# Scores of the diagonal packed into whole PSUM banks, products with V in four batches a group, eight slots for the weights

## The reference

```
mod = silu(c) @ wmod -> sa, ca, ga, sb, cb, gb          (ga, gb pushed away from zero)
h   = layernorm(x) * (1 + ca) + sa
x   = x + ga * (softmax_causal(Q K^T / 4) V @ Wo^T + bo)     with Q, K, V = h @ Wqkv^T + b
h   = layernorm(x) * (1 + cb) + sb
x   = x + gb * sum over the 2 chosen experts e of w_e * (silu(h @ w1[e]) @ w2[e])
```

## Time and profile before

| | |
|---|---|
| median of 3 runs | 999.07 us |
| span of the profiled execution | 997.7 us |
| TensorE busy (matmuls) | 902.3 us, 90% |
| VectorE busy | 718.0 us, 72% |
| ScalarE busy | 580.5 us, 58% |
| GpSimd busy | 357.4 us, 36% |

### The profile page before, as it was taken

One profiled execution on the slowest core, in us unless ns is written; L12 is line 12 of the kernel. 1 busy time (PEld: TensorE's weight loads), 2 busy tenths in 40 slices (PEclk: granted clock), 3 DMA queues, 4 the chain that ended last, 5 costly groups with the idle time before them and its releaser, 6 DMA issues.

```text
span 997.7 us, 19445 instructions
## 1 busy us (share of the span) xinstructions
PE 902.3 (90%) x6174; PEld 531.5 (53%) x6174; DVE 718.0 (72%) x2323; ACT 580.5 (58%) x1271; POOL 357.4 (36%) x311
## 2 busy tenths in 40 slices
PE   5899899999899998999999897878899999999990
PEld 3543335433444443543443452423699899999980
DVE  8688766879656789757689669699638584444587
ACT  3335485776585777577666757567535433334562
POOL 1332020431321314333033454015386466565630
PEclk7899899999999999999999999999999999999995
DMA  8446436336326167251662745215313323222699
GB/s 282 127 65 129 61 81 144 59 44 146 63 35 133 42 112 142 69 76 59 106 115 85 152 64 189 73 27 174 96 53 123 95 70 106 78 75 71 198 309 306
DMA packets 83235, 110.61 MB, mean 111 GB/s; under 512 B 15930, under 2 KB 56434, under 8 KB 83138
## 3 DMA queue, kind: packets, MB, share of 16 engines
q1 hardware_dynamic: 75506, 89.45, 38.8%
q0 software_dynamic: 6816, 18.62, 6.1%
q10 hardware_dynamic: 816, 1.32, 0.4%
HBM read 69.42 MB, written 35.41 MB: 105 GB/s over the span
## 4 chain that ended last, share of the span: by engine, by line
PE 62%; DVE 16%; ACT 9%; issue 5%; DMA 4%; POOL 3%; SPq 1%; ACTq 0%; POOLq 0%; DVEq 0%
PE PO L1643 10%; PE PH L1520 9%; PE PY L1520 9%; PE PS L1623 8%; PE PM L1600 8%; ACT PR L1009 4%; DVE MXF L1322 3%; PE PHT L1728 3%; PE PX L1655 2%; PE PX L1569 2%; DVE JK L1319 2%; PE PS L1627 2%; PE PX L1578 2%; PE PX L1579 1%; ACT SF L992 1%
## 5 line engine op out<-in xcount | busy, mean ns | idle before, releaser
L1009 ACT ACTIVATE PR<-PS 128x512 f32<-128x512 f32 (+3 forms) x768 | 334.3, 497 | 142.4 <-PE PS L1627 108.1
L1319 DVE CUSTOM_DVE_ANT_0 JK<-PM,MK 128x128 bf16<-128x128 f32 (+3 forms) x512 | 239.1, 484 | 54.0 <-PE PM L1600 52.8
L1600 PE MATMUL PM<-QK 128*128 128x512 bf16 (+3 forms) x768 | 249.1, 333 | 23.4 <-DVE MXF L1322 15.0
L1623 PE MATMUL PS<-QK 128*128 128x512 bf16 (+3 forms) x768 | 247.5, 333 | 10.4 <-ACT PR L1009 7.4
L1322 DVE TENSOR_REDUCE MXF<-PM 128x1 f32<-128x512 f32 x256 | 175.1, 684 | 83.2 <-PE PM L1600 81.6
L1623 PEld LDWEIGHTS PS<-QK 128*128 128x128 bf16 x768 | 75.0, 98 | 170.4 <-ACT PR L1009 107.8
L1643 PE MATMUL PO<-PR,V 128*17 128x512 f32 (+3 forms) x1536 | 162.8, 496 | 0.0
L1600 PEld LDWEIGHTS PM<-QK 128*128 128x128 bf16 x768 | 75.5, 99 | 98.0 <-DVE MXF L1322 36.8
L1520 PE MATMUL PY<-W2S,HT 128*128 x852 | 118.9, 289 | 2.8 <-issue 1.9
L1520 PE MATMUL PH<-W1S,XT 128*128 x426 | 113.3, 402 | 0.9 <-DVE W2S L1474 0.9
L1627 PE MATMUL PS<-MT,identb 128*128 128x128 bf16 x512 | 111.9, 221 | 0.0
(11 more groups left out here) (269 smaller groups left out, 1194.9 us busy)
## 6 DMA issues: line engine op xcount, KB each, us to landing
QK<-SD SPq DMA_DIRECT2D x180, 128.0 KB
SD<-SP SPq DMA_DIRECT2D x42, 256.0 KB, 2.8
OP<-OS SPq DMA_DIRECT2D x64, 64.0 KB
LP<-LR SPq DMA_DIRECT2D x64, 64.0 KB
W1S<-in_w SPq DMA_DIRECT2D x8, 512.0 KB, 5.7
X<-XA SPq DMA_DIRECT2D x3, 1024.0 KB, 8.8
H2D<-XA SPq DMA_DIRECT2D x3, 1024.0 KB, 4.9
YG<-YT SPq DMA_DIRECT2D x12, 256.0 KB, 4.4
```

Of the source, the lines that this page charges most:

```text
L1009: eng.activation(PR[:, slot, i, c0:512], PS[m % 3][:, c0:512], ACT.Exp, scale=0.25).then_inc(S["exp"].sem, 1)
L1319: eng.tensor_tensor_reduce(JK[:, jk % 2, 0:w], PM[m % 3][:, 0:w], MK[:, 512 - w:512], 1.0, -3.0e38, ALU.add, ALU.max, MXA[:, mb, h, qt:qt ...
L1600: eng.matmul(PM[m % 3][:, 0:128 * (k1 - k0)], QK[:, r, h, 0, qt * 128:(qt + 1) * 128], QK[:, r, h, 1, k0 * 128:k1 * 128], start=True, stop ...
L1623: last = eng.matmul(PS[m % 3][:, c0:512], QK[:, r, h, 1, j * 128:(j + 1) * 128], QK[:, r, h, 0, 512 * f + c0:512 * f + 512], start=True, s ...
```

## The change

Eight key blocks of a group's 12 hold diagonal parts, of 512, 384, 256 and 128 columns a head. The change lists, for each half f: the key blocks up to 4f as before ("all", 512 columns); a slot kind "odd", whose bank holds a head's 384 columns of key block 4f+1 and behind them its 128 columns of block 4f+3; and a kind "two", whose bank holds the 256 columns of block 4f+2 for two heads. So a group has 18 slots (36 banks) in place of 24 (48 banks), and every exponential has 512 columns. The mask of "odd" and "two" is one matmul of 256 columns (for "two" with an output of two strips of 128). Score step n of a group stands where half step 48n/36 stands, maxima stay where they are. The products with V are made in 4 steps a group: key blocks 0 to 3 of half 0; blocks 0, 1 of half 1; blocks 2, 3; blocks 4 to 7. Each step waits once, for the last exponential of its batch, and stands LAG steps after its last score (steps 9, 14, 19 and 26 from the group's start; before, the 12 stood 2 steps apart at 4 to 26). `PR` has 8 slots, the last three at another place in SBUF; for their space the reserve for GpSimd's DMA descriptors is set to 4096. The unused `LATE` is taken out.

```diff
-SLOTS = 5
+SLOTS = 8
+FIRST_SLOTS = 5
-SCORES = [(f, j, p) for f in range(2) for j in range(4 * f + 4) for p in range(2)]
+SCORES = [slot for f in range(2) for slot in
+          [("all", f, j, p) for j in range(4 * f + 1) for p in range(2)] + [("odd", f, 1, p) for p in range(2)] + [("two", f, 2, 0)]]
+BATCHES = ((0, 5, (0, 1, 2, 3)), (5, 9, (0, 1)), (9, 13, (2, 3)), (13, 18, (4, 5, 6, 7)))
+def score_pieces(n, i):
+    kind, f, j, p = SCORES[n]
+    if kind == "all":
+        return [(2 * p + i, j, 0, 512, 0)]
+    if kind == "odd":
+        return [(2 * p + i, 4 * f + 1, 128, 512, 128), (2 * p + i, 4 * f + 3, 0, 128, 384)]
+    return [(2 * i, 4 * f + 2, 0, 256, 256), (2 * i + 1, 4 * f + 2, 256, 512, 256)]
...
-        for n, (f, j, p) in enumerate(SCORES):
-            if p == 1:
-                place(g, n + LAG - ahead(g, f), one("pv", g, f, j))
+        for n, (_, f, _, _) in enumerate(SCORES):
+            k = half_of("score", 2 * n + 1) // 2 - ahead(g, f)
+            b = batch_of(n)
+            if n == BATCHES[b][1] - 1:
+                place(g, k + LAG, one("pv", g, b))
...
# ScalarE, score
-                    if m // 2 >= SLOTS:
-                        ac.wait_ge(S["pv"], (m // 2 - SLOTS) // 2 + 1)
-                    eng.activation(PR[:, slot, i, c0:512], PS[m % 3][:, c0:512], ACT.Exp, scale=0.25).then_inc(S["exp"].sem, 1)
+                    if s >= SLOTS:
+                        ac.wait_ge(*after("pv", "pv", (s - SLOTS) // NS, batch_of((s - SLOTS) % NS)))
+                    eng.activation(PR[s % SLOTS][:, i, :], PS[m % 3][:, :], ACT.Exp, scale=0.25).then_inc(S["exp"].sem, 1)
...
# TensorE, score
-                    last = eng.matmul(PS[m % 3][:, c0:512], QK[:, r, h, 1, j * 128:(j + 1) * 128],
-                                      QK[:, r, h, 0, 512 * f + c0:512 * f + 512], start=True, stop=True)
+                    for piece, (h, j, c0, c1, q0) in enumerate(score_pieces(n, i)):
+                        q0 += 512 * f
+                        last = eng.matmul(PS[m % 3][:, c0:c1], QK[:, r, h, 1, j * 128:(j + 1) * 128],
+                                          QK[:, r, h, 0, q0:q0 + c1 - c0], start=piece == 0, stop=True, skip_group_check=True)
...
# TensorE, pv
-                    for i in range(4):
-                        last = eng.matmul(PO[32 * i:32 * i + 17, c0:512], V[g // 4 % 2][:, j, 4 * (g % 4) + i, :],
-                                          PR[:, (m - 1 + i // 2) % SLOTS, i % 2, c0:512], start=(j == 0), stop=(j == 4 * f + 3),
-                                          skip_group_check=True)
+                    for j in keys:
+                        for h in range(4):
+                            n, i, c0, c1, q0 = place_of(f, j, h)
+                            last = eng.matmul(PO[32 * h:32 * h + 17, q0:q0 + c1 - c0], V[g // 4 % 2][:, j, 4 * (g % 4) + h, :],
+                                              PR[ring_s["score", g, n, i] // 2 % SLOTS][:, i, c0:c1], start=(j == 0),
+                                              stop=(j == 4 * f + 3), skip_group_check=True)
...
-    nc = bacc.Bacc("TRN2", target_bir_lowering=False, num_devices=1)
+    nc = bacc.Bacc("TRN2", target_bir_lowering=False, num_devices=1, dynamic_dma_scratch_size=4096)
```

More of the change, by code:

```diff
@@ L83, in is_cut @@
 def is_cut(n):
-    f, j, _ = SCORES[n]
-    return j >= 4 * f
+    kind, f, j, _ = SCORES[n]
+    return kind != "all" or j == 4 * f
 def schedule():
@@ new lines, in schedule, with score_step, max_step @@
+    score_at = {half_of("score", n): n for n in range(2 * NS)}
+    def score_step(t, i):
+        w, k = divmod(t, nw)
+        if 1 <= w < NG and 2 * k + i in score_at:
+            n = score_at[2 * k + i]
+            return ("score", w, n // 2, n % 2)
+        for f in range(2):
+            n = score_at.get(2 * (t + AHEAD[f]) + i)
+            if n is not None and SCORES[n // 2][1] == f:
+                return ("score", 0, n // 2, n % 2)
+    def max_step(t, i):
+        g, m = divmod(t + LEAD, nw)
+        if 0 <= g < NG and 2 * m + i in max_at:
+            return ("max", g, max_at[2 * m + i])
@@ L227, in schedule @@
     for t in range(-3 * nw, NG * nw + LAG + 1):
         now[0] = t - 0.5
[L229 to L240, removed]
+        if score_step(t, 0):
+            order.append(score_step(t, 0))
+        elif (t + LEAD) // nw >= 0 and t < -AHEAD[0]:
@@ L247, in schedule @@
         now[0] = t
-        if score:
-            order.append(("score", *score, 1))
-        order += fill[1:]
+        if score_step(t, 1):
+            order.append(score_step(t, 1))
+        if max_step(t, 1):
+            order.append(max_step(t, 1))
         while at.get(t):
@@ L312 @@
 NR = len(ROUTE[0])
-LATE = ()
 RING = 10
@@ L502, in adaln_block @@
         TM = sb("TM", [128, 2, D], F32, att)
+        PRB = sb("PRB", [128, SLOTS - FIRST_SLOTS, 2, 512], F32, att)
+        PR = [PRA[:, i, :, :] for i in range(FIRST_SLOTS)] + [PRB[:, i, :, :] for i in range(SLOTS - FIRST_SLOTS)]
         GBO = TM[:, 0, :]
@@ L1625, in tensor_program @@
                     if is_cut(n):
                         pe.wait_ge(S["const"], 8)
-                        last = eng.matmul(PS[m % 3][:, c0:c0 + 128], identb[:, :], MT[:, :], start=False, stop=True,
-                                          skip_group_check=True)
+                        if SCORES[n][0] == "all":
+                            out_, mask = PS[m % 3][:, 0:128], MT[:, 0:128]
+                        elif SCORES[n][0] == "odd":
+                            out_, mask = PS[m % 3][:, 0:256], MT[:, :]
+                        else:
+                            out_ = PS[m % 3][:, :].rearrange("p (h q) -> p h q", h=2)[:, :, 0:128]
+                            mask = MT[:, :].rearrange("p (h q) -> p h q", h=2)
@@ L1629, in tensor_program @@
+                        last = eng.matmul(out_, identb[:, :], mask, start=False, stop=True, skip_group_check=True)
                     last.then_inc(S["st"].sem, 1)
                 elif kind == "pv":
-                    g, f, j = a
-                    c0 = 128 * max(0, j - 4 * f)
-                    n = SCORES.index((f, j, 1))
-                    m = ring_s["score", g, n, 1] // 2
-                    pe.wait_ge(*after("exp", "score", g, n, 1))
-                    pe.wait_ge(*after("v", "v", g // 4, j // 2))
@@ L1637, in tensor_program @@
-                    if j == 0 and (g, f) != (0, 0):
+                    g, b = a
+                    n0, n1, keys = BATCHES[b]
+                    f = int(b > 0)
+                    pe.wait_ge(*after("exp", "score", g, n1 - 1, 1))
+                    pe.wait_ge(*after("v", "v", g // 4, keys[-1] // 2))
+                    if b < 2 and (g, b) != (0, 0):
                         pe.wait_ge(S["os"], S["os"].before[step])
-                    elif j == 0:
+                    elif b == 0:
                         pe.wait_ge(S["po0"], 1)
```

78 lines of the change are left out of this document (42 added, 36 removed).

## The result

The changed kernel takes 1030.23 us (median of 4 runs, 1028.69 to 1033.12), the kernel before beside it 998.92: a ratio of 1.032, 95% interval 1.030 to 1.034. It is slower, as forecast, but by 31 us in place of 11, above the range of 980 to 1024.

What follows compares the result with a forecast made beforehand. TensorE was taken to pace, with VectorE close behind and taking over in groups without projections. Window changes summed to +11 us on the 997.7 us span, 1008.7, plus 1.4 for the median: 1010 us, range 980 to 1024.

Steps and rivals of the forecast that it cites:

- Part 1: Twelve product steps a group become four: 128 steps fewer, 0.21 us each, 26 us saved on TensorE.
- Part 2: VectorE idles behind each long batch, 1.3 to 1.7 us, 6.0 us a group; by windows the sum is +11 us.
- Part 4: Exponentials, 768 become 576: ScalarE saves 33 us beside TensorE's work, counted as 0.
- Part 5: Slots, waits for exponentials, GpSimd's descriptor reserve, wider mask constant and moved buffers: 0 us; reserve +6 us at worst.
- Rivals A: Whole kernel faster: TensorE's saving shows, VectorE's idle falls where it would have waited anyway; about 984 us, chance 0.29.
- B: No change: idle only 1.0 to 1.2 us a batch, VectorE work lies between the blocks; 999 us, chance 0.12.
- Rival D: Masks spaced wider than their columns, 1000 us; chance 0.02.
- 285 to 329 us and its two likes: Windows with many projections: TensorE gains 1.7 us and loses it in its maxima stretch without projections; 0.
- Part 3: Packed scores and masks: equal columns, 192 matmuls fewer worth 0 to 2 us, strided output at worst 7 us; taken as 0.
- 605 to 652 us: Window where VectorE (38.0 of 47 us) and TensorE (39.1) hold each other up: +1.5 us.
- 652 to 702 us: Window after the last maxima: saving of 11 steps, 2.3 us, and lighter ScalarE show in full, -3 us.
- Rival C: Slower by more: idle 1.95 us a batch, also beside projections, and late maxima for next group's scores; 1025 us, chance 0.09.

Runs made afterwards that it cites:

- 2: Changed kernel's packed scores, but products with V in ten steps a group, none over 512 columns, against the kernel before: 1008.09 us, 1.009.
- 10: Kernel with unpacked scores and twelve product steps, each half a step earlier than in the kernel before: 998.33 us, 0.999.
- 5: Packed scores with ten short product steps, each half a step earlier, against the kernel before: 1002.38 us, 1.004.
- 4: Changed kernel with each batch of products half a step earlier; against the kernel before: 1021.39 us, 1.023.
- 9: Changed kernel with four PSUM banks for maxima and two for scores, in place of three and three: 1029.99 us, 1.030 to the kernel before.
- 7: Changed kernel with VectorE reducing only 128 columns of each block for query tiles from 4 on, exponentials' scale 0.05: 976.44 us, 0.976 to the kernel before.
- experiment 1: Changed kernel with scores unpacked and twelve one-block product steps again; slots, their place, reserve and mask constant stay changed: 999.36 us, 0.999 to the kernel before.
- the repeats: Edit in four runs: 29 score blocks made three times over in groups 13 and 14; on the changed kernel 1029.8 us, on the kernel before 1004.42 us.
- 14: Changed kernel with batches half a step earlier and 29 score blocks made three times over: 1019.22 us, 1.018 to the kernel before.
- 13: Changed kernel with 29 score blocks made three times over, batches at whole steps: 1029.8 us, 1.027 to the kernel before.
- 11: Unpacked scores, six product steps of two key blocks, each half a step earlier, against the kernel before: 1010.32 us, 1.009.
- light kernels: Kernels where VectorE reduces only 128 columns of each maxima block for query tiles from 4 on: kernel before 976.98 us, changed one 976.44 us.
- 15: Changed kernel with lighter maxima for VectorE and 29 score blocks made three times over: 978.26 us, 0.976 to the kernel before.
- 6: Kernel before with VectorE reducing only 128 columns of each block for query tiles from 4 on, exponentials' scale 0.05: 976.98 us, 0.978.

## Why the prediction was wrong in size

The direction and the main mechanism were right; the forecast failed by three terms that it set at 0.

*What held.* Part 1: over 77 to 640 us the distances between starts, less what the columns take, give 0.10 us lost in front of a product step and 0.11 behind it before, 0.11 and 0.12 after, and next to nothing between the key blocks of a batch. 163 steps became 53, so TensorE is spared some 110 x 0.2 = 22 us there; for all 128 steps fewer that is an estimate of 26 us, as forecast. Part 2, the mechanism: VectorE starves behind a batch. Groups without projections are longer by 2.4 us each (forecast 2.0), the kind of 358 to 396 us by 1.0 (forecast 1.3); VectorE's idle until maxima went from 134 to 162 us (forecast 170). The same distances in front of a maxima matmul, where TensorE waits for a bank, went from 31 to 66 us. That the 2.4 us came out so near is partly luck: packing with ten short steps (2) already has 1.2 of it (91.1 us for the three groups against 87.4), and the forecast gave packing nothing. At half steps the batches have most of it (10, 5 and 4: 86.6, 87.8 and 93.3 us). With four maxima banks, or light maxima, most or all of the loss goes (experiments 9, 7). Part 4: the exponentials went from 334 to 317 us on ScalarE in all, and saved no time; of the 33 us I took them for, half came. Part 5: 0, shown by experiment 1 for the slots, their place, the reserve and the mask constant. Rivals A and B are out: VectorE had no work in hand through a batch. Rival D (masks spaced wider than their columns, 1000 us) is out by the time: a mask of 256 columns holds TensorE for 0.11 us (198.39 to 198.50), one of 128 for 0.06 (195.03 to 195.09). By the Trainium skill, TensorE: Matmul & The Clock Gate, Back-to-back issue gap, 128 columns want about 81 ns in a stream of weight load and matmul pairs; this trace doesn't agree, and the measurement decides.

*What failed.* Three terms that I set at 0: batches beside projections, packing, and TensorE's clock. Four ratios lay them out, each a step from the kernel before to the changed one:

| from, to | ratio | us |
|---|---|---|
| before, to packing with ten short steps, half a step early (5) | 1 to 1.0035 | 3.5 |
| to four batches in their place, with the repeats and so little low clock in the router's groups (14) | to 1.0184 | 15 |
| to batches at whole steps, beside projections (13) | to 1.0272 | 9 |
| to TensorE at the low clock in groups 12 to 14 (the changed kernel) | to 1.0321 | 5 |

Each ratio is known to about 0.0025, so each difference to some 3 us; the last two rows have a second pair each (4 against the changed kernel: 0.0095; 14 against 4: 0.0042). The second row changes two things, since 5 has 17 us at the low clock in 600 to 740 us and 14 has 3.4; without repeats on either side (4 against 5) the batches cost 0.0191, 19 us.

1. *Part 2, beside projections: "285 to 329 us and its two likes: 0", and 0.8 us for 396 to 445.* Measured 0.9 and 3.0 us a group. I took a projection stretch for a place where TensorE's gain shows. A batch that stands right behind a projection makes one stretch of 4 to 6 us without maxima, against three banks of 0.51 us. Two pairs give the price of the move off the whole steps: 9 us from 4 to the changed kernel, 9 us from 14 to 13. In the traces groups 1, 4, 5, 8 and 9 have 5.4 us of it (4 against the changed kernel) and 5.7 us (229.0 to 223.3, 14 against 13), so the place beside projections is shown for a little over half. With ten short steps the move gives 5 us and none in these groups, unpacked it gives 0. The pairs of maxima (experiments 10 and 11) would explain why it needs packing: 12 a group become 5 with ten steps, and TensorE's distances in front of maxima matmuls fall from 45 us (2) to 29 us (5). No run changes the pairs alone.
2. *Part 3, packing: 0.* Experiment 2 against 1 puts it at 9 us at whole steps, 5 against 10 at 4 us at half steps (in these two traces only 0.7 us of it stand before the first expert matmul, 704.6 against 703.9 us, so at half steps packing costs attention little or nothing). The columns are equal, as I said. What isn't equal is the order: 36 scores on 48 half steps stand between 48 maxima, so some maxima follow each other with nothing between. TensorE then asks for a bank sooner than VectorE frees one. Over 77 to 640 us the trace of 1 has 25 such pairs and that of 2 has 169; the distances beyond the columns are 7 us against 34 in front of these maxima, and 29 against 45 us in front of all. With 89 pairs (5) it is 29 us again, as unpacked (10: 24 pairs, 30 us). So the traces bear the mechanism out, but it is not isolated: no run spreads the scores otherwise, and 4.2 us of the loss of 2 stand in the router's groups, with more of the low clock.
3. *The clock: no term at all.* The earlier trace rows showed 0.96 in 605 to 652 us, so the trace of before had a stretch at the edge. TensorE was busy for 1.65 us of 614 to 618 us, the clock fell behind these waits, and a batch of 1024 columns at 1.2 GHz then starved VectorE for longer still:

```profile
648.31 1.91 PE L1702 MATMUL PO<-PRA,V 128*17 128x512 f32 x8
649.99 1.93 PE L1702 MATMUL PO<-PRB,V 128*17 128x512 f32 x8
651.86 0.54 PE L1675 MATMUL PS<-QK 128*128 128x384 bf16 x2
```

3.55 us, against 1.84 at 2.4 GHz. The price is 5 us net of the added matmuls, so at least that; by the three groups' lengths it is 139.2 - 128.5 = 10.7 us. "-3" for 652 to 702 us and "+1.5" for 605 to 652 us became +14 for groups 12 to 15.

The 15 to 19 us of the second row are what Part 2 was meant to be: the idle behind batches, 11 by the forecast. Rival C came nearest to the time (1025) with two mechanisms. The idle beside projections was right. The late chain to the next group's scores I didn't see in the waits.

*What stays open.* In the light kernels TensorE's saving of some 20 us (0.2 us for each product step fewer) doesn't show in the end. Groups 12 to 14 take 8 us of it (123.4 against 115.0), not by the clock (15). More waits for ScalarE stand around the projections; these rows are of 7, 77 to 664 us:

```profile
PE PS L1676 <- ACT PRB L1060: 9.4, 13, 1.6
PE PM L1652 <- DVE MXF L1375: 9.2, 9, 2.9
...
PE PX L1659 <- ACT SF L1044: 4.9, 3, 1.6
PE PX L1611 <- ACT hT L1028: 3.6, 6, 1.0
PE PX L1611 <- ACT XN L1022: 3.3, 4, 1.0
```

and of 6:

```profile
PE PS L1624 <- ACT PR L1009: 7.0, 16, 0.9
PE PM L1601 <- DVE MXF L1323: 5.6, 6, 2.6
...
PE PX L1608 <- ACT SF L992: 2.6, 3, 0.9
PE PX L1560 <- ACT hT L976: 1.9, 3, 0.8
...
PE PX L1560 <- ACT XN L970: 1.1, 4, 0.4
```

TensorE waits 4.9 + 3.6 + 3.3 = 11.8 us for ScalarE's copies `SF`, `hT` and `XN`, against 2.6 + 1.9 + 1.1 = 5.6, and 9.4 + 9.2 = 18.6 against 7.0 + 5.6 = 12.6 for exponentials (in 7 those of `PRB` alone) and full maxima. No experiment took these away. No version beats the kernel before: the best, 10, is at 0.999 with 1 inside its interval.

## What to carry to other kernels

Before joining short steps of the engine that paces, write down the longest stretch in which it will make nothing for the next engine, with the neighbours that the order gives it, and hold it against the work which that engine has in its ring. Here 2.3 us alone against 1.5 us cost 15 to 19 us of 1000, and the same batches at whole steps 9 more, some 5 of them where the projections stand. Equal columns don't make a packing free: after it, look for steps of one ring that now follow each other with nothing between. Where TensorE's clock already dips in the kernel before, more waiting there has a second price.

## What was not expected of the hardware

The granted clock fell to 0.50 at 618 us after 4 us in which TensorE was busy for 1.65, and stayed there for 10 us in which it was busy for 7.98. Matmuls whose results are thrown away held it at 1.00 in that stretch and made the program faster, by 0.5% and 0.4% in two pairs. Over the executions of one kernel a us more at the low clock went with 0.31 us more of span, less than the half that a TensorE without waits would lose. The changed kernel's runs have 25 us more at the low clock than those of the kernel before (mean clock 0.959 against 0.971), and the repeats give 5 us (net) to 10.7 us back. The Trainium skill, TensorE: Matmul & The Clock Gate, Terms, counts such time times a half, by which I estimate 12 us; the runs lie below it.
